# Routing list in two rounds, zero fills one expert tile later, and reordered layer openings in a four-layer transformer kernel

## The reference, cut to what matters

```python
def reference(x, cond, ...):          # x [4, 512, 288], cond [4, 288], float32
    x = L0(x)     # attention block with 16 heads, then a mixture of 4 experts, top 2
    x = L1(x)     # attention block, then a dense MLP
    x = L2(x)     # x + ((x U) R - x U) U^T, U = Q of a QR of P, R = expm(skew(cond))
    x = L3(x)     # attention block, then a dense MLP
    return x

# every attention block:
mod = silu(cond) @ w_ada + b_ada      # shift, scale, gate for attention and for the MLP
h = layernorm(x) * (1 + scale) + shift
attn = softmax(q @ k.T * 18 ** -0.5)
x = x + gate * (attn @ v @ w_proj + b_proj)

# experts of the first layer:
logits = xf @ w_gate; top2, softmax over the two
moe = sum over the two of cw * (gelu(xf @ w1[e] + b1[e]) @ w2[e] + b2[e])
x = x + gate * moe
```

## Time and profile before

| | us |
|---|---|
| Median of 3 runs | 1723.29 (1721.15 to 1725.44) |
| The profiled execution: its own time | 1734.02 |
| The profiled execution: span from the first to the last instruction | 1732.3 |
| TensorE busy in it | 1588.6 |
| VectorE busy | 1098.9 |
| ScalarE busy | 942.3 |
| GpSimd busy | 610.3 |

### The profile page before, as it was taken

One profiled execution on the slowest core, in us unless ns is written; L12 is line 12 of the kernel. 1 busy time (PEld: TensorE's weight loads), 2 busy tenths in 40 slices (PEclk: granted clock), 3 DMA queues, 4 the chain that ended last, 5 costly groups with the idle time before them and its releaser, 6 DMA issues.

```text
span 1732.3 us, 27974 instructions
## 1 busy us (share of the span) xinstructions
PE 1588.6 (92%) x9537; PEld 1036.3 (60%) x9537; DVE 1098.9 (63%) x2236; ACT 942.3 (54%) x1696; POOL 610.3 (35%) x1349
## 2 busy tenths in 40 slices
PE   7899989899889999997789999999988999998998
PEld 5434445446778888886334454479864454543897
DVE  4857767656544546474777877544457878784544
ACT  2456546566655555563356657744433767676442
POOL 1256665556255546663465643110001002101100
PEclk9799989999999999998789999999998999999999
DMA  6643533414384355441432223220203323222000
GB/s 199 197 131 94 162 108 120 165 59 164 115 266 131 121 196 161 158 145 49 148 112 88 88 62 94 73 60 1 47 25 117 107 88 93 69 76 73 18 28 28
DMA packets 102480, 183.45 MB, mean 106 GB/s; under 512 B 13581, under 2 KB 55960, under 8 KB 102226
## 3 DMA queue, kind: packets, MB, share of 16 engines
q1 hardware_dynamic: 91598, 145.98, 27.0%
q0 software_dynamic: 8352, 33.20, 6.2%
q10 hardware_dynamic: 2388, 2.48, 0.5%
HBM read 133.18 MB, written 60.05 MB: 112 GB/s over the span
## 4 chain that ended last, share of the span: by engine, by line
PE 67%; DVE 14%; DMA 6%; ACT 6%; issue 4%; SPq 2%; POOL 1%; another core or an unknown queue 0%; DVEq 0%; ACTq 0%; POOLq 0%
PE ps L1339 13%; PE ps L1350 13%; PE ps L1195 8%; PE ps L1184 7%; DVE mx L2047 6%; PE ps L1073 6%; PE ps L1124 4%; PE ps L1171 3%; PE ps L1080 2%; DMA w2raw<-in_w 2%; PE ps L1113 2%; PE ps L1094 1%; ACT pT L1633 1%; PE ps L1087 1%; SPq L480 1%
## 5 line engine op out<-in xcount | busy, mean ns | idle before, releaser
L2047 DVE TENSOR_REDUCE mx<-ps 128x1 f32<-128x512 f32 x768 | 481.6, 681 | 71.3 <-PE ps L1171 63.4
L1633 ACT ACTIVATE pT<-ps 128x512 f32<-128x512 f32 x768 | 411.0, 603 | 194.6 <-PE ps L1184 182.9
L1171 PE MATMUL ps<-ks,qs 54*128 54x512 f32 x768 | 298.6, 484 | 25.9 <-DVE mx L2047 8.5
L1184 PE MATMUL ps<-qs,ks 56*128 56x512 f32 x768 | 274.5, 457 | 20.6 <-issue 5.7
L1981 DVE TENSOR_TENSOR gl<-gf,gh 128x512 fp32r<-128x512 f32 x171 | 118.8, 695 | 195.9 <-ACT gh L1547 194.7
L1184 PEld LDWEIGHTS ps<-qs,ks 56*128 56x128 f32 x768 | 117.4, 189 | 184.4 <-issue 101.4
L1195 PE MATMUL ps<-pT,vaug 128*32 128x512 f32 x1536 | 211.9, 620 | 6.6 <-ACT pT L1633 6.6
L1350 PE MATMUL ps<-w2h,gh 128*128 128x288 f32 x684 | 206.7, 302 | 4.5 <-DVE tmp L2324 2.5
L1350 PE MATMUL ps<-w2l,gh 128*128 128x288 f32 x684 | 201.9, 295 | 0.0
L1350 PE MATMUL ps<-w2h,gl 128*128 128x288 f32 x684 | 201.4, 294 | 0.0
L799 POOL TENSOR_SCALAR nwp<-mvp 128x4 f32<-128x4 f32 x21 | 4.1, 197 | 520.2 <-DVE mvp L1866 519.8
(11 more groups left out here) (293 smaller groups left out, 3041.7 us busy)
## 6 DMA issues: line engine op xcount, KB each, us to landing
qk_rows<-qk SPq DMA_DIRECT2D x96, 252.0 KB
w1raw<-in_w SPq DMA_DIRECT2D x39, 576.0 KB, 4.3
ks<-qk_rows SPq DMA_DIRECT2D x288, 72.0 KB
w2raw<-in_w SPq DMA_DIRECT2D x39, 432.0 KB, 4.9
qs<-qk_rows SPq DMA_DIRECT2D x96, 144.0 KB
expert_out<-expert_out POOLq DMA_DIRECT2D x8, 1152.0 KB, 6.0
htok<-expert_rows SPq DMA_DIRECT2D x11, 768.0 KB, 6.8
qs<-qk_rows SPq DMA_DIRECT2D x96, 72.0 KB
```

Source lines behind the costliest of these rows:

```text
L1171: ins = mm(bank(n), qs[at:at + KMAX, buf, h // 2, qt * P:(qt + 1) * P], ks[at:at + KMAX, buf, h // 2, :], start=True, stop=True, tile_posi ...
L1184: ins = mm(bank(n), ks[at:at + KROW, b % 2, h // 2, kt * P:(kt + 1) * P], qs[at:at + KROW, b % 2, h // 2, :], start=True, stop=True, tile_ ...
L1633: A(pT[:, kt % 2 * HG + i, :], bank(BANK[when[0], "score", (g, kt, i)]), ACT.Exp, scale=SCALE).then_inc(S["exp_done"], 1)
L2047: V.tensor_reduce(mx[:, g % NG, qt, column(i):column(i) + 1], bank(BANK[when[0], "max", (g, qt, i)]), AX.X, ALU.max).then_inc(S["mx_done"], 1)
```

## The change

- The list of row 3 is made in two rounds: `pick_tiles(3, 4, True)` picks tile 3 as a full one, then, after `tl_ready` 3, `pick_tiles(4, 11, False)` picks the other seven. The last list is now `tl_ready` 4.
- SP loads the tokens of tile 3 at the head of round 3, after `tl_ready` 3. The zero fills stand in round 3 (during tile 2), one behind piece 0, two behind piece 1, one behind piece 2. The load that waits for them is that of tile 4 (`WHOLE`), in round 4 behind piece 0.
- Tokens are turned at places 5, 7 and 8 in all tiles.
- The q and k stacks are laid out in plain blocks, q as high, low, high and k as high, high, low, with six loads of 18 rows for each, twelve in all. It holds for every unit of every layer.
- In the opening the k half of stack 0 is issued by ScalarE, behind high part 1 and a wait for the stores of tiles 0 and 1; SP issues the q half.
- The gates are made behind the max tiles (0, 0) and (0, 3), in `l` 0 and 2.
- VectorE takes the statistics of the next unit before low parts 2 and 3.

```diff
-def token_places(k):
-    return (6, 7, 8) if k == PICKED[2] - 1 else (5, 7, 8)
+WHOLE = PICKED[2] + 1
+TOKEN_PLACES = (5, 7, 8)
...
+GATES_AT = ((0, 0), (0, 3))
...
-FILL_AT = ((0, 1), (2,), (3,))
+FILL_AT = ((0,), (1, 2), (3,))
...
-STACK_LOADS = 2 * 5 * 16
+STACK_LOADS = 2 * 6 * 16
...
 def load_rows(eng, i, g, which):
...
-                both = heads[e].rearrange("d a p n -> (d a) p n")
-                for at, step, src in ((0, 1, both), (2 * HD, 1, high)) if to is qs else ((0, 2, high), (1, 2, high), (2 * HD, 1, low)):
-                    rows = src.shape[0]
-                    start = HALF * e + at
-                    eng.dma_start(to[start:start + step * (rows - 1) + 1:step, i % 2, 2 * g:2 * g + 2, :].bitcast(F32), src).then_inc(S[f"stack_ld{g}"], 16)
+                for k, src in enumerate((high, low, high) if to is qs else (high, high, low)):
+                    at = HALF * e + HD * k
+                    eng.dma_start(to[at:at + HD, i % 2, 2 * g:2 * g + 2, :].bitcast(F32), src).then_inc(S[f"stack_ld{g}"], 16)
...
-                stack(B * l, 0)
+                stack(B * l, 0, (0,))
...
-                        if k != PICKED[2]:
+                        if k == PICKED[2]:
+                            sp.wait_ge(S["tl_ready"], 3)
+                        if k != WHOLE:
                             load_tokens(k)
...
-                        if (k, q) == (PICKED[2], 0):
+                        if (k, q) == (WHOLE, 0):
                             sp.wait_ge(S["zf_done"], NE * 16)
                             load_tokens(k)
-                        for n in FILL_AT[q] if k == PICKED[2] - 1 else ():
-                            sp.wait_ge(S["tl_ready"], 3)
+                        for n in FILL_AT[q] if k == PICKED[2] else ():
+                            sp.wait_ge(S["tl_ready"], 4)
...
 # TensorE, start(); banks() takes its banks in the same order
-                        for u in range(2):
-                            modulation_gate(l, u, bank_free("G", (l, u), "gate_cp", 2 * l + u + 1))
                     for g in range(2):
                         for qt in range(TT):
                             max_tiles(g, qt, range(HG))
+                            if l != 1 and (g, qt) in GATES_AT:
+                                u = GATES_AT.index((g, qt))
+                                modulation_gate(l, u, bank_free("G", (l, u), "gate_cp", 2 * l + u + 1))
...
 # ScalarE, start()
-                    for tile in range(QT - 1):
+                    for tile in range(2):
+                        high_part(it, tile)
+                    for tile in range(2):
+                        act.wait_ge(S[f"qk_st{tile}"], stored(it, tile))
+                    load_rows(act, it, 0, 1)
+                    for tile in range(2, QT - 1):
                         high_part(it, tile)
...
 # VectorE, start()
-                    for tile in range(2, QT - 1):
-                        low_part(it, tile)
-                    if l != 1:
-                        modulation_half_out(l, 1, BANK[when[0], "M", (l, 1)])
...
                     for part in "abc":
                         statistics(1, it + 1, b + 1, part)
+                    for tile in range(2, QT - 1):
+                        low_part(it, tile)
+                    if l != 1:
+                        modulation_half_out(l, 1, BANK[when[0], "M", (l, 1)])
...
 # VectorE, tile_list(b)
+                if b < B - 1:
+                    pick_tiles(PICKED[b - 1], PICKED[b], True)
+                else:
+                    pick_tiles(PICKED[b - 1], WHOLE, True)
+                    dve.wait_ge(S["tl_ready"], 3)
+                    pick_tiles(WHOLE, PICKED[b], False)
```

More of the change, by code:

```diff
@@ L204, in banks @@
             take(phase, "M", (l, 1))
-            for u in range(2):
-                take(phase, "G", (l, u))
         for g in range(2):
@@ L210, in banks @@
                     take(phase, "max", (g, qt, i))
+                if l != 1 and (g, qt) in GATES_AT:
+                    take(phase, "G", (l, GATES_AT.index((g, qt))))
                 if (g, qt) == (1, 0):
@@ L910, in _ @@
                         pool.wait_ge(S["zf_done"], NE * 16)
-                        pool.wait_ge(S["tl_ready"], 3)
+                        pool.wait_ge(S["tl_ready"], 4)
                         gather(1)
@@ L1383, in expert_tile @@
                     late((k, j, "A"))
-                    if j in token_places(k) and k + 1 < TILES:
-                        c = token_places(k).index(j)
+                    if j in TOKEN_PLACES and k + 1 < TILES:
+                        c = TOKEN_PLACES.index(j)
                         spare_free(reads, "hs_done", KC * (k + 1) + c + 1)
@@ L1750, in expert_tile @@
                     late((k, j, "A"))
-                    if j in token_places(k) and k + 1 < TILES:
-                        input_high(k + 1, token_places(k).index(j), SPARE)
+                    if j in TOKEN_PLACES and k + 1 < TILES:
+                        input_high(k + 1, TOKEN_PLACES.index(j), SPARE)
                     if j in FWD_TILE[k]:
@@ L2260, in tile_list @@
             def tile_list(b):
-                first, n, pad = PICKED[b - 1], PICKED[b] - PICKED[b - 1], 8
-                whole = b + 1 < B
-                def flat(t):
-                    return t.rearrange("p t e -> p (t e)")
                 if b == 1:
@@ L2270, in tile_list, with pick_tiles, flat @@
                 dve.wait_ge(S["pos_read"], b + 1)
+                if b < B - 1:
[4 more added lines that the diff above has]
+                    pick_tiles(WHOLE, PICKED[b], False)
+            def pick_tiles(first, end, whole):
+                n, pad = end - first, 8
+                def flat(t):
+                    return t.rearrange("p t e -> p (t e)")
                 tk_step(V.memset(tlp[:, :, :], 0.0))
@@ L2274, in tile_list @@
                                                scalar=-float(N if whole else 1), in1=tstart[0:1, :, :], op0=ALU.add, op1=ALU.is_ge))
-                if b > 1:
+                if first:
                     tk_step(V.tensor_tensor(need, need, flat(taken[:, :, :]), ALU.subtract))
@@ L2282, in tile_list @@
                                                    op0=ALU.is_equal, op1=ALU.mult), q == n - 1)
-                if b == 1:
+                if not first:
                     tk_step(V.tensor_copy(flat(taken[:, :, :]), flat(tpick[:, 0, :, :])))
-                if b == 2:
+                elif whole:
                     for q in range(n):
@@ L2293, in tile_list @@
                 tk_step(V.tensor_scalar(tgot[:, 0:n, 2], tgot[:, 0:n, 2], float(IDLE), None, ALU.add))
-                if b == B - 1:
+                if not whole:
                     tk_step(V.tensor_copy(total[:, :], count[0:1, :]))
@@ L2348, in expert_tile @@
                     late((k, j, "A"))
-                    if j in token_places(k) and k + 1 < TILES:
-                        input_low(k + 1, token_places(k).index(j), SPARE)
+                    if j in TOKEN_PLACES and k + 1 < TILES:
+                        input_low(k + 1, TOKEN_PLACES.index(j), SPARE)
                     if k and j == 1:
```

## The result

The changed kernel is slower: 1727.47 us (median of 20 runs, 1717.91 to 1730.87) against 1719.86 us for the kernel before (20 runs beside it, 1713.94 to 1726.05), ratio 1.0035, 95% interval 1.0022 to 1.0048. By the ratio that is 6.0 us more (the two medians lie 7.6 apart) where the prediction had 4.2 less, and the median lies outside the predicted range, 1711.5 to 1727, by 0.5 us. The profiled execution of after took 1728.82 us (span 1727.1), a typical one; the one of before took 1734.02, 14 us above its median, so the two spans must not be compared as they stand. I compare stretches instead.

A forecast was written before the change was run, and what follows sets the result against it. The prediction took TensorE to bound the kernel, so only its waits, or VectorE holding it, could pay. Terms: expert phase +3.4, openings -2.6, -2.0, -2.0, other stacks -1.0, sum -4.2 us, 1719.1 on the median; range 1711.5 to 1727.

The forecast's parts named there:

- What bounds the kernel: Whole kernel: the chain runs 67% over TensorE, so the change pays only where TensorE waits or VectorE holds it.
- Tile k = 2: Expert phase, third tile: token stop and its slow clock go, fills leave the crowded stretch; -6.4 us, ends -1.5 and -6.7.
- Tile k = 3: Expert phase, next tile: the token stop moves here, 6.8 us, plus 2.2 of low clock; +9.0 us.
- The list: Expert phase, tile 1: two rounds add about 2.7 us on VectorE, mostly covered; +0.8 us, ends 0 and 2.7.
- Layer 0's opening: Max tiles start at 38.49 instead of 43.93, ahead of the gates; -2.6 us, ends 2.1 and 3.5 of gain.
- Layer 1's opening: Plain k loads on two queues land earlier, at near 219 GB/s; -2.0 us, ends 0.5 and 3.4 of gain.
- Rival 2: Openings: transfer over fewer engines bounds the loads, gaining 0.5 in layers 1 and 2; sum +0.3 us, 1723.6, chance 0.20.
- Layer 2's opening: The load gives the same gain as in layer 1, now that the gates no longer cover it; -2.0 us.
- All other stacks: Attention stages: cheaper k issues on SP shorten waits for the rows of maxima; -1.0 us, ends 0 and -2.5.
- 3: Expert phase: token stop is paid twice and it loses more than the openings gain; +8.9 us, 1732.2, chance 0.08.
- a quarter of 0.47: Whole kernel: the forecast itself had chance 0.47, a quarter of it lying beyond -5.2 us.
- the chance of "faster": Whole kernel: chance 0.37 of a gain beyond 0.3% (5.2 us), from 0.20, 0.14 and a little more.

The follow-up runs named there:

- e_fills: Changed kernel with the zero fills back during tile 1 and the tokens of tile 4 at the head of round 4; 0.9978 of the kernel before.
- e_expert: Kernel before with only the expert part of the change (two-round list, early tile 3 tokens, later fills, token places 5, 7, 8); 1.0085 of the kernel before.
- e_openings: Kernel before with everything of the change except its expert part; 0.9964 of the kernel before.
- e_before: Kernel before, run again with no edit for a second profile; its profiled execution took 1740.0 us, 25 runs beside it had a median of 1735.4.
- e_before_head: Kernel before with the tokens of tile 3 loaded at the head of SP's round 3, behind the last zero fill; 1.0052 of the kernel before.

## Why the prediction was wrong

- **What bounds the kernel**: right as far as the traces go; what was found or lost in the expert phase are stops of TensorE and its clock behind them.
- **Tile k = 2, the step that failed.** The prediction said: "The fills leave the crowded stretch", and "I take 1.5, since the scatter and a large modulation load stay there. Sum -6.4." The stop for tokens did go, 4.9 us with its clock. But the load did not stay there: it follows the scatter's landing, which the fills and the short list had kept late. It moved onto a weight piece. Measured: a stop of 7.1 where the slow piece of before had cost 0.6, and (3.22 - 1.60) + (2.78 - 1.63) = 2.8 of low clock; less 4.9 it is +4.4. With 0.5 for the list it is 4.9, and the step to tile 3 shows +5.1. That term is off by some 11 us, about the whole error of the forecast (10.2 by the ratio). All bounds of it (-1.5 to -6.7) were gains. The prediction also took the crowding of before for one piece of 6.66 us; the next one, of 9.6, stands in no row of it.
- **Tile k = 3**: +9.0 forecast, 5.5 of stop and 2.70 - 1.60 = 1.1 of clock, with the tail +7.2. Right in kind, a little dear.
- **The list**: +0.8 forecast, at the token turn of place 7. Measured 0.5 net there and at place 8, so right in kind and size; its consequence (the fills wait for it, e_fills) was missed.
- **Layer 0's opening**: -2.6 forecast; 52.1 and 51.9 us became 49.7, and 49.0 to 51.3 over all profiles with the new order. About 2, so nearly right in size. Two things in it were not: the load on two queues ended at 39.66, not near 38, and TensorE stood 2.4 us for it; and the gain hangs on the clock of the old order (51.9 to 52.7 us in four of its profiles, 48.6 in e_expert).
- **Layer 1's opening**: -2.0 forecast; 48.5 us became 48.8 (e_openings 49.0). The step that failed is "I take 2.0, close to the measured rate": the rate of 219 GB/s belonged to a stretch with loads of 36 rows in it, and plain ones alone ran at 131 to 152. Rival 2 came nearest with its 0.5, and its cause, fewer engines, fits the share of 0.58 to 0.61.
- **Layer 2's opening**: -2.0 forecast. Before it took 50.7 where the gates ran at the full clock (3.08 us) and 55.8 where they ran near 1.2 GHz (5.76); with the change 53.2, and 50.4 to 53.5 over all profiles with it. So the gain depends on which clock before had, and the first profile had the good one: the four others with the old order took 55.4 to 55.8. Against those the change gains 2 to 5 us, against the first it gains nothing.
- **All other stacks**: k issues of 0.32 us (forecast 0.35), and the waits for the maxima's rows 3.0 shorter. Everything outside the experts gave 6 us (0.9964), where the terms said 7.6, though less of it from the openings.
- **The rivals**: 3 had the sign and the point from which it decides (the expert phase loses more than the openings gain), but not the cause; its chance of 0.08 was too small since nothing in my sum asked what a scatter without fills would release. Forecast and rivals were also weighed loosely: a quarter of 0.47 is 0.12, not the 0.14 that the chance of "faster" was given.

## What to carry to other kernels

When traffic is taken out of a queue, ask what was waiting behind it: here an edit that looked like a pure relief let a load of 1.9 MB start 4 us sooner against the tile's work, right beside a weight piece. Large loads of two queues belong in each other's gaps, in parts that fit there, and a wait of the issuing engine must be checked against the work that stands in front of it. A load's rate is that of its own shape; a window in which wider loads fly says nothing of narrow ones.

## What was not expected of the hardware

- A piece of weights (576 + 432 KB) lands in 4.9 us by the median. With 1.9 MB of another queue issued at most 5 us before it or with it, it took 11.1 to 14.4 us (six profiles; 12.98 in after), with fills ahead of it as well 14.46, and with 1 MB ahead of it 7.85 and 8.10. With the load 7 us ahead and a fill behind it, as in before, it took 9.6.
- The same code took 77.5 us from the fifth q and k tile of layer 1's first unit to that of the second in e_before, and 66.2 in e_before_head on another chip; the granted clock over the stretch differs (windows, 0.83 and 0.89):

```profile
830.00:920.00 90.00, 75.54 (x359) 33.48 (x358) 69.38 (x123) 46.94 (x85) 45.25 (x38) 0.83 0.40 117
```

```profile
830.00:920.00 90.00, 81.42 (x426) 37.73 (x426) 76.81 (x140) 52.71 (x98) 53.07 (x70) 0.89 0.45 135
```

So two profiles can differ by 10 us in a stage that no edit touched, which is as large as the effects looked for here; the expert phase (411.8 to 418.1 with its code unchanged) was steadier. Its own spread is still 6 us, so a difference of 5 us in it counts here only where the stop that explains it is seen to come or go.
